# Tile 4 takes two weight blocks side by side in one matmul of 512 columns, and the weight blocks are split in another order

## What is computed

```
u = x @ root + bias
for r in range(8):
    mask   = (edge_type == r)
    sums   = segment_sum(x[src] * mask, dst);  cnt = segment_sum(mask, dst)
    u     += (sums / max(cnt, 1)) @ weight[r]          # 1024 x 1024 per relation
z = concat([u, x]) @ w_gate + b_gate
h = tanh(u) * z + x * (1 - z)
x = layernorm(x + h)
```

## Time and profile before

| | |
|---|---|
| median of three runs | 834.55 us |
| the profiled execution's own time | 834.18 us |
| its span, first to last instruction | 832.4 us |
| TensorE (PE) busy | 816.1 us, 98% |
| VectorE (DVE) busy | 672.2 us, 81% |
| ScalarE (ACT) busy | 443.5 us, 53% |
| granted TensorE clock, mean | 0.999 of full speed |
| matmuls of `seven` | 3888, of 256 columns |
| matmuls of `aggregate` | 800, of 512 columns |

### The profile page before, as it was taken

The page is one execution under the profiler, slowest core; times in us unless marked ns, Lnnn a source line. Parts: engine busy times, 40 slices in busy tenths (PEclk is TensorE's granted clock), DMA queues, the critical chain, the costliest instruction groups (busy, mean ns, idle before and its releaser), DMA issues.

```text
span 832.4 us, 15910 instructions
## 1 busy us (share of the span) xinstructions
PE 816.1 (98%) x6324; PEld 586.0 (70%) x6324; DVE 672.2 (81%) x949; ACT 443.5 (53%) x621; POOL 14.6 (2%) x32
## 2 busy tenths in 40 slices
PE   7999999999999999999999999999999999999996
PEld 5566755468776867768678686786867868768544
DVE  8999798998977777677776777867678677788897
ACT  6888788267555355353553545625446254445711
POOL 1000000000000000000000000000000000000000
PEclk9999999999999999999999999999999999999999
DMA  9622658202220120211202102022020220305811
GB/s 317 115 38 27 216 173 196 102 4 99 103 102 33 70 102 1 101 48 53 101 0 101 66 34 101 0 101 85 16 101 0 101 100 3 128 1 152 202 51 73
DMA packets 60214, 71.06 MB, mean 85 GB/s; under 512 B 30692, under 2 KB 34400, under 8 KB 60173
## 3 DMA queue, kind: packets, MB, share of 16 engines
q1 hardware_dynamic: 59297, 69.64, 26.9%
q10 hardware_dynamic: 876, 0.85, 0.4%
HBM read 57.96 MB, written 5.18 MB: 76 GB/s over the span
## 4 chain that ended last, share of the span: by engine, by line
PE 89%; DVE 6%; ACT 3%; DMA 1%; issue 1%; SPq 0%; DVEq 0%
PE psP L1246 51%; PE psA L1317 21%; PE psP L1043 12%; PE psA L1024 2%; PE psP L996 1%; ACT cu_mem L706 1%; DVE p_mem L1549 1%; PE psP L1052 1%; DVE vec L1465 1%; ACT wsplit L739 1%; DVE p_mem L1548 1%; ACT wsplit L690 1%; ACT dump L617 1%; DMA stage<-in_src 0%; DVE cu_mem L1688 0%
## 5 line engine op out<-in xcount | busy, mean ns | idle before, releaser
L1246 PE MATMUL psP<-wsplit,xT 128*128 128x256 f16 x2592 | 294.6, 273 | 0.0
L1246 PEld LDWEIGHTS psP<-wsplit,xT 128*128 128x128 f16 x2592 | 253.6, 98 | 33.0
L1317 PE MATMUL psA<-p_mem,cu_mem 128*128 128x512 f16 x800 | 175.3, 379 | 0.0
L1246 PE MATMUL psP<-wsplit,x 128*128 128x256 f16 x1296 | 150.3, 273 | 0.0
L1317 PEld LDWEIGHTS psA<-p_mem,cu_mem 128*128 (+1 forms) x800 | 78.3, 98 | 90.9 <-DVE cu_mem L1818 0.2
L1246 PEld LDWEIGHTS psP<-wsplit,x 128*128 128x128 f16 x1296 | 126.8, 98 | 14.7
L1510 DVE SCALAR_TENSOR_TENSOR wsplit<-stage,sc,wsplit 128x1024 f16<-128x1024 f32 x90 | 114.7, 1279 | 27.0 <-ACT wsplit L701 27.0
L701 ACT ACTIVATE wsplit<-stage,sc 128x1024 f16<-128x1024 f32 x90 | 100.6, 1137 | 16.1 <-DVE sc L1385 10.5
L1818 DVE SCALAR_TENSOR_TENSOR cu_mem<-psA,coef,cu_mem 128x512 f32<-128x512 f32 x80 | 60.0, 750 | 31.5 <-PE psA L1317 30.1
L701 ACT ACTIVATE wsplit<-x,sc 128x1024 f16<-128x1024 f32 x54 | 61.7, 1144 | 42.0 <-PE psP L1246 31.1
L1510 DVE SCALAR_TENSOR_TENSOR wsplit<-x,sc,wsplit 128x1024 f16<-128x1024 f32 x54 | 69.2, 1282 | 10.2 <-ACT wsplit L701 9.8
(11 more groups left out here) (223 smaller groups left out, 797.2 us busy)
## 6 DMA issues: line engine op xcount, KB each, us to landing
stage<-in_L_gnn_weight SPq DMA_DIRECT2D x16, 2048.0 KB, 7.9
stage<-in_L_gnn_w_gate SPq DMA_DIRECT2D x4, 2048.0 KB, 8.2
x_home<-x SPq DMA_DIRECT2D x5, 512.0 KB, 3.0
x<-x_home SPq DMA_DIRECT2D x5, 512.0 KB, 6.9
x<-in_x SPq DMA_DIRECT2D x4, 512.0 KB, 8.2
xT<-in_L_gnn_root SPq DMA_DIRECT2D x1, 2048.0 KB, 9.2
stage<-in_L_gnn_root SPq DMA_DIRECT2D x1, 2048.0 KB, 7.9
out<-x SPq DMA_DIRECT2D x4, 512.0 KB
```

Source lines behind the costliest of these rows:

```text
L1246: last = nc.tensor.matmul(psP[:, bank, (col + tt) * FB:(col + tt + 1) * FB], lhs[tt](a, c), split_block(n, b)[:, c, :], start=(first and t ...
L1317: last = nc.tensor.matmul(psA[:, (NT * h + t) % 2, :], cnt8[:, r, s, t * P:(t + 1) * P], p_part[h][a][:, s, :], start=(s == 0 and a == 0), ...
```

## The change

From unit 1 to unit 16 tile 4's four parts of 12 matmuls of 256 columns become two parts of 12 matmuls of 512 columns (`wide`): one with B11 and B12 side by side, in the place where B12 stood, and one with B21 and B22, at the end of the unit. Unit 0 and unit 17 keep the narrow form (`narrow`).

So the slots of B11 and B21 are used until late in a unit. The splits for unit 2 and after are written in the order T2, T1, T3, T4, B11, B12, B21, B22 (`ORDER`; before: B11, T2, B21, T1, T3, T4, B12, B22), on ScalarE, on VectorE and in TensorE's waits (`split_at`, `free_at`). The splits for unit 0 and unit 1 keep the old order. `third_diff` now makes T3, and `fourth_diff` makes T4 in its own buffer instead of over raw B21. VectorE's work for unit 0 is written out by itself; before unit 0 the third sum is made behind the last `root_out` instead of before the third. For units 16 and 17 the same orders are used in the written-out gate part. Cut to its core:

```diff
--- before.py
+++ after.py
...
@@ -414,11 +414,25 @@
             if n in (T1, T3):
                 return t_block(0)
-            if n == T2:
+            if n in (T2, T4):
                 return t_block(1)
-            return raw_block(i, slot, *{B11: (0, 0), B12: (0, 1), B21: (1, 0), B22: (1, 1), T4: (1, 0)}[n])
-        TDIFF = {T1: 1, T2: 2, T4: 3, T3: 4}
+            return raw_block(i, slot, *{B11: (0, 0), B12: (0, 1), B21: (1, 0), B22: (1, 1)}[n])
+        TDIFF = {T1: 1, T2: 2, T3: 3, T4: 4}
+        FIRST_ORDER = (B11, T2, B21, T1, T3, T4, B12, B22)
+        ORDER = (T2, T1, T3, T4, B11, B12, B21, B22)
+        FREE = {B11: 7, T2: 2, B21: 8, T1: 4, T3: 5, T4: 6, B12: 7, B22: 8}
+        def split_at(j, n):
+            return (FIRST_ORDER if isinstance(j, int) and j < 2 else ORDER).index(n) + 1
+        def free_at(j, n):
+            return n + 1 if isinstance(j, int) and j == 1 else FREE[n]
         def scale_col(i, slot):
             return i if i <= U_WO else 2 + slot
...
@@ -879,35 +893,50 @@
                 act.wait_ge(prod, STEPS * j + 1)
                 nc.scalar.activation(p1_tmp, bank(0), ACT.Copy, scale=PROD1_GAIN).then_inc(p1_ready, 1)
                 act.wait_ge(scale_step, 3 * (j + U_REL + 1) + 3)
-                step_high(j + 1, 1 - slot, 0)
-                step_high(j + 1, 1 - slot, 1)
+                if sums_first:
...
+                    return
+                step_high(j + 1, 1 - slot, T2)
                 act.wait_ge(prod, STEPS * j + 3)
                 if settled:
                     act.wait_ge(agg_full, NT * (j - 1))
                 high(hi[:, 0:2, 0:FB], bank(0), PROD1_GAIN)
-                step_high(j + 1, 1 - slot, 2)
-                step_high(j + 1, 1 - slot, 3)
-                if sums_first:
-                    weight_sum(j + (U_REL + 2), slot, loads, parts=(0, 1))
+                step_high(j + 1, 1 - slot, T1)
+                step_high(j + 1, 1 - slot, T3)
                 act.wait_ge(c22_ready, j + 1)
                 high(hi[:, 2:4, FB:HALF], c22[:, :, :])
-                if sums_first:
-                    weight_sum(j + (U_REL + 2), slot, loads, parts=(2, 3))
-                    act.wait_ge(prod, STEPS * (j + 1))
-                    high(hi[:, 4, :], psP[:, 4, :], PROD1_GAIN)
-                step_high(j + 1, 1 - slot, 4)
+                step_high(j + 1, 1 - slot, T4)
                 act.wait_ge(c21_ready, j + 1)
                 high(hi[:, 2:4, 0:FB], p1_tmp)
-                step_high(j + 1, 1 - slot, 5)
-                if not sums_first:
-                    act.wait_ge(prod, STEPS * (j + 1))
-                    high(hi[:, 4, :], psP[:, 4, :], PROD1_GAIN)
+                step_high(j + 1, 1 - slot, B11)
+                step_high(j + 1, 1 - slot, B12)
+                act.wait_ge(prod, STEPS * (j + 1))
+                high(hi[:, 4, :], psP[:, 4, :], PROD1_GAIN)
                 act.wait_ge(c12_ready, j + 1)
                 high(hi[:, 0:2, FB:HALF], p16_tmp)
-                step_high(j + 1, 1 - slot, 6)
-                step_high(j + 1, 1 - slot, 7)
-                if not sums_first:
-                    weight_sum(j + (U_REL + 2), slot, loads)
+                step_high(j + 1, 1 - slot, B21)
+                step_high(j + 1, 1 - slot, B22)
+                weight_sum(j + (U_REL + 2), slot, loads)
             rel_step(0, 0, slot_load(U_REL + 2), settled=False, sums_first=True)
             rel_step(1, 1, slot_load(U_REL + 3), settled=False)
...
@@ -1257,7 +1286,19 @@
                 S3, S2, S4 = range(3)
                 Z, X, Y, W, V = range(NT)
-                b0 = weight_blocks(U_REL + j)
+                def ready(n):
+                    blocks_ready(weight_blocks(U_REL + j) + split_at(j, n))
+                def wide(k, n0, n1, start, stop=False):
+                    for c in range(KB):
+                        for a, b in ((0, 0), (0, 1), (1, 0)):
+                            last = nc.tensor.matmul(psP[:, V, :].rearrange("p (k f) -> p k f", k=2),
+                                                    xT[:, a, k * KB + c, (NT - 1) * P:NT * P],
+                                                    wsplit[:, n0:n1 + 1:n1 - n0, b, c * FB:(c + 1) * FB],
+                                                    start=(start and c == 0 and a == 0 and b == 0),
+                                                    stop=False, skip_group_check=True)
+                    return last
                 if first:
                     pe.wait_ge(root_done, NT + 1)
...
@@ -1265,47 +1306,52 @@
                     pe.wait_ge(zx_done, 1)
                 else:
                     pe.wait_ge(p_lo, 5 * (j - 1) + 1)
-                blocks_ready(b0 + 1)
-                part(B11, Z, 0, x_tiles(0, 0, 1), True)
-                if second:
-                    pe.wait_ge(p167_ready, j)
-                    blocks_ready(b0 + 2)
-                    part(T2, X, 0, s_tiles(S2), True)
+                narrow = first or gate
+                ready(B11)
+                last = part(B11, Z, 0, x_tiles(0, 0, 1), True)
                 if first:
                     pe.wait_ge(root_done, 2 * NT)
-                elif not gate:
-                    pe.wait_ge(p_lo, 5 * (j - 1) + (3 if second else 4))
-                part(B11, V, 0, x_tiles(0, 4), True).then_inc(prod, 2 if second else 1)
+                if narrow:
+                    last = part(B11, V, 0, x_tiles(0, 4), True)
+                last.then_inc(prod, 1)
                 if first:
                     pe.wait_ge(s_lo, 3)
                 else:
                     pe.wait_ge(p167_ready, j)
-                if not second:
-                    blocks_ready(b0 + 2)
-                    part(T2, X, 0, s_tiles(S2), True).then_inc(prod, 1)
-                blocks_ready(b0 + 3)
-                part(B21, V, 0, x_tiles(1, 4), False)
+                ready(T2)
+                part(T2, X, 0, s_tiles(S2), True).then_inc(prod, 1)
+                ready(B21)
+                if narrow:
+                    part(B21, V, 0, x_tiles(1, 4), False)
                 pe.wait_ge(p1_ready, j + 1)
                 part(B21, Z, 0, x_tiles(1, 0, 1), False).then_inc(prod, 1)
                 if first:
                     pe.wait_ge(s_lo, 4)
                 else:
                     pe.wait_ge(c12_ready, j)
-                blocks_ready(b0 + 4)
+                ready(T1)
                 part(T1, Y, 0, x_tiles(0, 2, 3), True).then_inc(prod, 1)
-                blocks_ready(b0 + 5)
+                ready(T3)
                 pe.wait_ge(p16_ready, j + 1)
                 part(T3, X, 0, s_tiles(S3), False).then_inc(prod, 1)
-                blocks_ready(b0 + 6)
+                ready(T4)
                 if not first:
                     pe.wait_ge(c21_ready, j)
                 part(T4, W, 0, x_tiles(1, 2, 3), True).then_inc(prod, 1)
-                blocks_ready(b0 + 7)
-                part(B12, V, 1, x_tiles(0, 4), False).then_inc(prod, 1)
-                blocks_ready(b0 + 8)
+                ready(B12)
+                if narrow:
+                    part(B12, V, 1, x_tiles(0, 4), False).then_inc(prod, 1)
+                else:
+                    pe.wait_ge(p_lo, 5 * (j - 1) + (3 if second else 4))
+                    wide(0, B11, B12, True).then_inc(prod, 1)
+                ready(B22)
                 pe.wait_ge(c22_ready, j + 1)
-                part(B22, Y, 0, s_tiles(S4), False)
-                part(B22, V, 1, x_tiles(1, 4), False).then_inc(prod, 1)
+                last = part(B22, Y, 0, s_tiles(S4), False)
+                if narrow:
+                    last = part(B22, V, 1, x_tiles(1, 4), False)
+                else:
+                    last = wide(1, B21, B22, False)
+                last.then_inc(prod, 1)
             def aggregate(j, r, h, first=False):
                 pe.wait_ge(p_lo, 5 * (j + 1))
...
@@ -1853,49 +1898,61 @@
                     sum_16()
                 unit_scale(j + (U_REL + 1), 1 - slot, REL)
                 first_diffs(j + 1, 1 - slot)
-                step_low(j + 1, 1 - slot, 0)
+                if isinstance(j, int) and j == 0:
+                    step_low(1, 1, B11)
+                    step_low(1, 1, T2)
+                    rest(1, low_rows, left, bank(0), PROD1_GAIN)
+                    step_low(1, 1, B21)
+                    sum_22()
+                    step_low(1, 1, T1)
+                    third_diff(1, 1)
+                    fourth_diff(1, 1)
+                    rest(2, high_rows, right, c22[:, :, :])
+                    dve.wait_ge(prod, 6)
+                    stt(p1_tmp, bank(3), PROD1_GAIN, p1_tmp, ALU.mult, ALU.add).then_inc(c21_ready, 1)
+                    rest(3, 4, slice(0, HALF), psP[:, 4, :], PROD1_GAIN)
+                    step_low(1, 1, T3)
+                    rest(4, high_rows, left, p1_tmp)
+                    dve.wait_ge(prod, STEPS)
+                    dve.wait_ge(p16_ready, 1)
```

(112 more changed lines are left out.)

6 lines of the change are left out of this document (4 added, 2 removed).

## The result

837.81 us median of 7 runs (837.24 to 838.01), the kernel before 834.55 (834.18 to 835.73): ratio 1.0037, 95% interval 1.0027 to 1.0046, that is 2.3 to 3.8 us slower. The forecast was 837.2. The profiled execution's span is 836.2 us (832.4 before).

The account below looks back on a forecast made before the run. TensorE's own instructions were taken as the bound; 2.35 (unit 1) + 1.20 (aggregation) - 0.92 (savings) = +2.63 us gave 836.8 for the profiled execution, 837.2 us with the median's 0.37; range 835.7 to 840.4.

Parts of the forecast that it names:

- The saving: Repeated units: one 512-column matmul replaces two narrow ones, 0.0025 us less a pair, 0.06 us a unit.
- The wait in unit 1: Before B21 into Z, TensorE waits 2.41 us for ScalarE's copy, no longer covered; unit 1 ends 2.35 us later.
- Aggregation(0): Behind unit 1, third and fourth tiles wait 0.26 and 0.94 us for VectorE's adds: plus 1.20 us, bounds 0 and 2.4.
- The repeated units: In their aggregations the first add is done just before the third tile is due: no wait, 0.2 us left.
- The moved sum before unit 0: VectorE's work for unit 0 comes about 1.14 us later, taken up by a 1.57 us wait for ScalarE: no cost.
- rival D: TensorE's 2.4 us idle in unit 1 halves its granted clock, adding 5.2 us: 842.4 us; chance 4%.
- Rivals A: VectorE gets through the new order in time in unit 1, leaving only the copy's wait: 836.0 us; chance 15%.
- B (waits in the repeated units): Ordinary units' aggregations wait too, 0.2 to 0.4 us a unit over 15 units: 840 to 843 us; chance 15%.
- C (copy ready in time): In unit 1 ScalarE's copy is ready when TensorE arrives, so only the savings stay: 833.6 us; chance 8%.
- E (faster streaming): Wide matmuls stream faster than 0.2158 us each, saving 33 us: 801 us; chance 1%.

Follow-up runs that it names:

- e2: The changed kernel with both of VectorE's aggregation adds for unit 1 put ahead of B11's low split: 836.49 us, ratio 1.0025 to the kernel before.
- e6: The changed kernel with B12's low split ahead of the first aggregation add in units 2 to 15: 852.0 us, ratio 1.0209 to the kernel before.
- e1: The changed kernel with tile 4's four narrow parts kept in their old places in unit 1: 837.21 us, ratio 1.0036 to the kernel before.
- the changed kernel's second: The profile from running the changed kernel again with no edit: 837.98 us, ratio 1.0039 to the kernel before.
- e8b: e2 once more without a further edit, one profiled execution: 837.48 us.

## Why the prediction was right

- **The saving**: 0.0025 us a pair, 0.06 a unit. Shown by the period, 34.31 against 34.37, and back to 34.37 with narrow parts in the same places. The 131 ns of the Trainium skill, TensorE: Matmul & The Clock Gate, section "Back-to-back issue gap", had no part in it.
- **The wait in unit 1**: forecast 2.41 from the end of T2's matmuls, start to start, and 2.35 in the units' length; measured 208.17 - 205.69 = 2.48 (209.21 less the 1.04) and 2.42. The 2.32 in brackets is the same wait, counted from the end of the last matmul's way through the array. TensorE resumed 0.15 us behind the copy (208.49 + 0.57 = 209.06 to 209.21), where the prediction had 0.06, taken from a release by VectorE.
- **Aggregation(0)**: forecast +1.20, measured +1.17, and gone with the adds ahead (e2).
- **The repeated units**: forecast no wait and 0.2 us of room. The changed kernel's aggregations are 10.79 us, and e6 measured the room.
- **The moved sum before unit 0**: cost nothing behind unit 0's start; in both profiles of the changed kernel the copy started 30.58 us behind it, 30.59 before.
- **What the sum hid**: I added the two losses of unit 1 as if each had its own cause. The total is right, because the end of the second add was worked out from VectorE's own rows and TensorE's restart from that. But it was set by the chain of ScalarE and VectorE from unit 2's scale to the second add alone: with the copy's wait gone it is the same (e1). Had I proposed to cover the copy as the remedy, I would have won nothing. The sum's split into 2.35 and 1.20 is thus right as a description of where TensorE stands idle and wrong as a list of causes.
- **The clock** (rival D, 4%): it happens, in some executions. The row of 20 us at 1.00 did not exclude it. Its price was wrong too: 5.2 us were put down for it, and 48 matmuls took 1.66 us more, since the clock was back at 1.00 before they ended. In the changed kernel it costs 0.5 of the 1.66 us it takes from TensorE, the rest lies beside VectorE's chain. Trace and medians differ by 0.6 us (2.69 against 3.26, interval 2.3 to 3.8); executions with the fall can give at most 0.5 of that, how many there were is not shown, and the rest is open.
- Rivals A (adds in time in unit 1), B (waits in the repeated units), C (copy ready in time) and E (faster streaming) are out by the same rows: 11.96, 10.79, 2.32 and 34.31 us.

## What to carry to other kernels

Before adding up waits that a new order brings, follow the chain of the other engines to the last of them. If that chain does not depend on the first wait, its end alone sets the time, and removing the first wait only lengthens the next (e1). A new steady-state order should be tried on the first units separately: here the same saving costs 2.7 us when it begins in unit 1, which has no aggregation before it, and nothing when it begins one unit later. Where a written order leaves 0.2 us of room, an edit that puts 1.2 us of VectorE's work ahead of the add costs 1.04 us in each unit (e6).

## What was not expected of the hardware

A TensorE idle stretch of 2.3 us was followed by a granted clock of about half in two of the nine profiles of kernels with that wait (the changed kernel's second, and e8b) and in none of the others, for 1.56 and 1.66 us more time over the next 48 matmuls. In the first of the two TensorE resumed at 208.19 and the clock fell at 209.2; in e8b it resumed at 208.40 and the clock had fallen at 208.2, in the wait's last 0.2 us. It was back at 1.00, with the matmuls running, at 212.7 and 211.7. So one wait of the same length has two prices from execution to execution, and a single profile shows only one of them. Why it falls in some executions only is not shown.
